# One graph layer with a routed expert layer on one core: the edge sort in four chunks instead of two, positions computed on TensorE, unpadded edge tiles in a ring of 32 buffers with a (tile, block) table, the loops unrolled, and the last row additions made in the output tensor

## The reference

```
xl   = layernorm(x)                                  # x: 3125 x 256, f32
msg  = edge_weight[:, None] * xl[dst]                # 50,000 edges; dst is sorted, src is random
aggr = segment_sum(msg, src, 3125) + (1 + eps) * xl
h    = relu(relu(aggr @ W1 + b1) @ W2 + b2)
x1   = x + normalize(h) * scale + offset
out  = x1 + sum over the two best of 8 experts e of gate_e *
       (gelu(layernorm_e(x1) @ W1_e + b1_e) @ W2_e + b2_e)      # 256 -> 1024 -> 256
```

## Time and profile before

| | |
|---|---|
| median of 3 runs | 1497.83 us (1496.9 to 1498.81) |
| profiled execution, its own time | 1508.24 us |
| span of its trace | 1506.4 us |
| PE / PEld / DVE / ACT / POOL busy | 70% / 50% / 60% / 42% / 51% |
| first edge operation on DVE | 30.08 us |
| first gather | 251.74 us |
| first product of the graph matmuls | 986.69 us |
| start of the last copy's issue | 1493.66 us |

### The profile page before, as it was taken

How to read it: one execution, slowest core, us unless ns; L and a number is a source line. 1 busy time by engine, 2 the same in 40 slices (tenths; PEclk the granted TensorE clock), 3 DMA queues, 4 the chain that set the end, 5 groups by cost and what they waited for, 6 DMA issues and landing times.

```text
span 1506.4 us, 32386 instructions
## 1 busy us (share of the span) xinstructions
PE 1051.3 (70%) x7511; PEld 757.7 (50%) x7512; DVE 899.1 (60%) x2569; ACT 639.5 (42%) x2228; POOL 774.2 (51%) x755
## 2 busy tenths in 40 slices
PE   0003997667667676665665565799549999999994
PEld 0003665445545555333433343478437777777773
DVE  1999997556556666454645455558674545455552
ACT  0633997666666665111111111145244444444441
POOL 3762665555555554666666666532172444434341
PEclk9999998998998989566667666589569999999997
DMA  3020001222222224243434343812211222222224
GB/s 101 23 92 0 0 0 57 77 84 77 79 81 74 79 82 65 84 133 115 136 109 139 115 132 109 180 24 88 94 42 34 38 43 39 43 39 44 39 42 103
DMA packets 61925, 110.50 MB, mean 73 GB/s; under 512 B 11155, under 2 KB 43905, under 8 KB 61828
## 3 DMA queue, kind: packets, MB, share of 16 engines
q0 software_dynamic: 31872, 72.39, 20.5%
q1 hardware_dynamic: 30020, 37.73, 7.8%
HBM read 92.86 MB, written 20.42 MB: 75 GB/s over the span
## 4 chain that ended last, share of the span: by engine, by line
PE 57%; DVE 17%; issue 14%; another core or an unknown queue 5%; DMA 3%; DVEq 2%; SPq 1%; POOL 1%; ACT 0%; POOLq 0%; ACTq 0%
PE bank L613 17%; PE bank L605 10%; PE bank L751 7%; PE bank L738 4%; PE bank L740 4%; PE bank L739 3%; PE bank L753 3%; DVE RA L1230 2%; PE bank L639 2%; DVE Sw L1219 2%; PE bank L693 2%; PE bank L683 1%; DVE RB L1183 1%; DVE Wall L1069 1%
## 5 line engine op out<-in xcount | busy, mean ns | idle before, releaser
L507 POOL DMA_INDIRECT gbuf<-xl_d,idx_slot x440 | 435.4, 990 | 293.8 <-issue 101.1
L613 PE MATMUL bank<-gbuf,Sw 128*128 128x256 f32 x880 | 356.3, 514 | 251.6 <-issue 168.7
L613 PEld LDWEIGHTS bank<-gbuf,Sw 128*128 128x128 f32 x880 | 177.6, 243 | 365.6 <-issue 340.4
L1230 DVE TENSOR_TENSOR RA<-RA,bank 128x256 f32 x440 | 184.3, 419 | 259.4 <-remote 87.8
L605 PE MATMUL bank<-RB 128*128 128x232 f16 (+1 forms) x1960 | 256.6, 270 | 8.3 <-POOL RB L494 2.8
L605 PEld LDWEIGHTS bank<-RB 128*128 128x128 bf16 (+1 forms) x1960 | 185.9, 103 | 78.7 <-issue 29.0
L850 ACT ACTIVATE RB<-RB,pay_slot 128x128 f32<-128x128 f16 x392 | 154.1, 393 | 126.1 <-DVE RB L1176 100.8
L556 POOL DMA_INDIRECT sum_d<-RA,slot_tok x56 | 88.6, 1582 | 204.5 <-DVE RA L1446 185.1
L1008 ACT ACTIVATE RA<-bank,b1T 128x128 f32<-128x128 f32 x448 | 128.0, 368 | 97.6 <-PE bank L740 96.6
L740 PE MATMUL bank<-RA,Wall 128*128 128x128 f16 x896 | 167.2, 223 | 0.0
L738 PE MATMUL bank<-RA,Wall 128*128 128x128 f16 x896 | 166.4, 223 | 0.5 <-issue 0.4
(11 more groups left out here) (225 smaller groups left out, 1570.0 us busy)
## 6 DMA issues: line engine op xcount, KB each, us to landing
stage<-in_L_ffn_W SPq DMA_DIRECT2D x16, 1024.0 KB
gbuf<-xl_d,idx_slot POOLq DMA_INDIRECT x440
out_dram<-sum_d SPq DMA_DIRECT2D x1, 3125.0 KB, 12.3
Wall<-in_x SPq DMA_DIRECT2D x1, 3072.0 KB
xl_d<-Wall SPq DMA_DIRECT2D x1, 3072.0 KB
RB<-in_x SPq DMA_DIRECT2D x1, 3072.0 KB
sum_d<-RB SPq DMA_DIRECT2D x4, 640.0 KB
xn_d<-RA SPq DMA_DIRECT2D x4, 640.0 KB
```

The lines of the kernel that those rows point to most:

```text
L507: pool.indirect_dma_start(out=gbuf[:, j, :], out_offset=None, in_=xl_d, in_offset=bass.IndirectOffsetOnAxis(ap=idx_slot[:, j:j + 1].bitcas ...
L613: mm(bank[5 + j % 2][:, 0:D], Sw[:, j % 4, :], gbuf[:, j, :], start=True, stop=True).then_inc(agg_mm, 1)
L1230: dve.tensor_tensor(a, a, bank[5 + j % 2][:, 0:D], ALU.add).then_inc(agg_added, 1)
```

## The change

Edges are loaded as 128 partitions of 390 values and a remainder column, 391 columns in all. They are cut in four chunks of 72, 96, 110 and 113 columns. Positions come from TensorE: it counts each column's one-hot (`column_counts`, one matmul of one column each), DVE scans the counts and spreads the start of each (column, block) on a diagonal (`spread`), and two matmuls for each group of 20 columns add what is above in the column and the start (`places`); DVE takes the maximum over the blocks. Tiles are no longer padded: a tile of 128 sorted edges may hold several blocks, and a block may span tiles. The pairs (tile, block) are numbered; a chunk of C tiles has SN = C + 24 steps at most, rounded to an even number, so there are 96 + 120 + 134 + 138 = 488 steps of `Sw`, product and addition, and 391 gathers. A table gives two steps (tile, block) in one word; DVE and PE each read it every other step and split it by division and remainder. `Sw` compares a node number against a sliding stretch of a long ramp (`iota_c`), so a row of another block gives zero.

Gathers go into a ring of 32 buffers. Records and table stay in `gbuf` and are read in place by registers; the slot copies of ACT are gone. DVE builds `Sw` three steps ahead (LEAD). Chunk c + 1 is sorted within the steps of chunk c (in its first 63, 87 and 101 steps), and the positions of chunk c + 2 are worked out there too. All of this is unrolled on every engine, with constant waits. DVE takes the layernorm moments of x (25 bn_stats), x is loaded and `xl` stored in five groups, 18 of x's 25 tiles are loaded again before the first gather and 7 after the last step. PREP2 is 3: of the W2 of experts 3 to 7, four are converted within the graph matmuls and one behind the slot tables. The 22 other conversions stand in chunk 3's steps. Rows are added directly in the output tensor, which has 128 spare rows, and the last copy is gone.

```diff
-    C0 = (EC - extra) // 2 // U * U
-    S0 = (C0 + extra + U - 1) // U * U
-    C1 = EC - C0
-    S1 = (C1 + extra + U - 1) // U * U
-    assert C1 == S0 and S1 <= 256
-    COLS, SLOTS, CSTART = (C0, C1), (S0, S1), (0, C0)
...
+    CH = (72, 96, 110, EC - 278)
...
+    SN = [(C + NB - 1 + 1) // 2 * 2 for C in CH]
...
+    RG = 20
+    RING = 32
+    LEAD = 3
+    SR = 8
+    BASE = NB + 1
...
-    PREP2 = (S1 // U - 1 - 2 * NE) // 2
+    PREP2 = 3
+    LATE = (4, 5, 6, 7, 3)
...
+        ring = f32view(Wall, 2 * w2f - RING * D, RING * D)
...
+            for a, t in ((src, e_key), (dst, e_idx), (edge_weight, ew)):
+                sp.dma_start(t[:, 0:EFULL], a[0:EFULL * P].rearrange("(p c) -> p c", c=EFULL)).then_inc(edges_in, 16)
...
+            for g in range(NT // G):
+                full = G - 1 if g == NT // G - 1 else G
+                at = g * G * P
+                sp.dma_start(x_in[:, G * g:G * g + full, :], x[at:at + full * P, :].rearrange("(t p) d -> p t d", p=P)
+                             ).then_inc(x_group[g], 16)
...
+            sp.wait_ge(xl_stored, 16 * (NT // G + 1))
+            sp.wait_ge(acc_set, NT // G)
...
+            sp.dma_start(x1[:, 0:XEARLY, :], x[0:XEARLY * P, :].rearrange("(t p) d -> p t d", p=P)).then_inc(x_early, 16)
...
+            sp.wait_ge(x1_cleared, 1)
+            sp.dma_start(x1[:, XEARLY:NT - 1, :], x[XEARLY * P:FULL, :].rearrange("(t p) d -> p t d", p=P)).then_inc(x_late, 16)
...
+                if g < len(LATE):
+                    sp.wait_ge(w_done, len(CONV) + 2 * g)
+                    load_w2(LATE[g])
...
-            sp.dma_start(out, sum_d[0:N, :]).then_inc(out_done, 16)
...
-            with pool.Fori(0, C0 // U) as i:
-                for j in HI_ON_POOL:
...
-                    pool.tensor_scalar(hi16[:, j, 0:S0], iota_h[:, 0:S0], pay_slot[:, j // HALF, j % HALF, 1:2], None,
...
+            pool.wait_ge(acc_set, NT // G)
+            pool.wait_ge(xl_stored, 16 * (NT // G + 1))
+            for c in range(NCH):
+                pool.wait_ge(recs_taken, c + 1)
...
+                        pool.wait_ge(agg_mm, SB[of] + min(t - RING - T0[of] + NB - 1, SN[of] - 1) + 1)
+                    pool.indirect_dma_start(
+                        out=ring[:, t % RING * D:(t % RING + 1) * D], out_offset=None, in_=xl_d,
+                        in_offset=bass.IndirectOffsetOnAxis(ap=rec_i[:, t:t + 1].bitcast(U32), axis=0),
+                    ).then_inc(gathered[t % RING], 16)
...
+            def column_counts(c, k):
+                pe.wait_ge(oh_built, sum(groups(j) for j in range(c)) + k + 1)
+                for t in group_cols(c, k):
+                    m = mm(ranks[0:NB, t:t + 1], e_oh[c % 2][:, t, :], one_h[:, 0:1], start=True, stop=True)
...
+                o = bank[4 + n % 2][:, 0:w]
+                mm(o, above_big[:, :], e_oh[c % 2][:, cols[0]:cols[-1] + 1, :].rearrange("p t b -> p (t b)"), start=True, stop=False)
+                mm(o, ones[0:NB, :], spread_d[n % 3][:, 0:len(cols), :].rearrange("p t b -> p (t b)"),
+                   start=False, stop=True).then_inc(place_mm, 1)
...
-                for k, left in enumerate((node[:, :, 1], node[:, :, 0], wt[:, :, 1], wt[:, :, 0], lo_rest[:, s, :])):
...
+                for j, left in enumerate((node[:, :, 1], node[:, :, 0], wt[:, :, 1], wt[:, :, 0], lo_rest[:, s, :])):
+                    m = mm(bank[j // 4][:, j % 4 * P:j % 4 * P + CH[c]], left, hi16[:, s, 0:CH[c]],
...
+            def ring_slot(c, i):
+                if i % 2 == 0:
+                    pe.wait_ge(steps_ready, c + 1)
+                    h = (SB[c] + i) // 2
+                    words[h] = pe.value_load(step_tab[0:1, h:h + 1], min_val=0, max_val=(BASE * CH[c]) ** 2 - 1)
+                word = words[(SB[c] + i) // 2]
+                tile = (word // BASE) % CH[c] if i % 2 == 0 else word // (BASE * CH[c] * BASE)
+                return (tile + T0[c]) % RING * D
+            def agg_step(c, i):
+                n = SB[c] + i
+                at = pe.snap(ring_slot(c, i))
+                pe.wait_ge(sw_built, n + 1)
+                if n >= 2:
+                    pe.wait_ge(agg_added, n - 1)
+                if i < CH[c]:
+                    t = T0[c] + i
+                    pe.wait_ge(gathered[t % RING], 16 * (t // RING + 1))
+                mm(bank[2 + n % 2][:, 0:D], Sw[:, n % 4, :], ring[:, bass.ds(at, D)], start=True, stop=True).then_inc(agg_mm, 1)
...
-                act.activation(xl[:, t, :], x_in[:, t, :], ACT.Copy, accum_out=mean1[:, t:t + 1]).then_inc(sums_done, 1)
...
-                        words(C0 + U * i + j, j, 1)
-                        words(C0 + U * i + j + 1, j + 1, 1)
...
-                link(dve.tensor_copy(cprev[:, 1:B], cum[:, 0:B - 1, T - 1]))
...
+            def column_hots(c, k):
+                cols = group_cols(c, k)
+                n, c0 = len(cols), T0[c] + k * RG
+                dve.tensor_tensor(e_oh[c % 2][:, cols[0]:cols[-1] + 1, :],
...
+                C = CH[c]
+                dve.wait_ge(col_counts, sum(groups(j) for j in range(c + 1)))
+                link(dve.tensor_tensor_scan(incl[:, 0:C], ones[0:NB, 0:C], ranks[0:NB, 0:C], 0.0, ALU.mult, ALU.add))
...
-                for b in range(B):
-                    m = dve.scalar_tensor_tensor(out=work[:, b, :], in0=cum[:, b, :], scalar=first[:, b:b + 1], in1=oh[:, b, :],
...
-                link(dve.tensor_reduce(pos, work.rearrange("p b t -> p t b"), AX_X, ALU.add))
...
+                link(dve.tensor_tensor(step_v[:, 0:S], row25[:, 1:1 + S], ranks[0:1, 192:192 + S], ALU.subtract))
...
+                link(dve.scalar_tensor_tensor(out=step_tab[:, SB[c] // 2:(SB[c] + S) // 2], in0=two[:, :, 1],
+                                              scalar=float(BASE * CH[c]), in1=two[:, :, 0], op0=ALU.mult, op1=ALU.add))
...
+                if n >= 3:
+                    dve.wait_ge(place_mm, n - 2)
+                dve.tensor_tensor(spread_d[n % 3][:, 0:w, :],
+                                  base[:, cols[0]:cols[-1] + 1].rearrange("p (t a) -> p t a", a=1).to_broadcast([NB, w, NB]),
...
+                dve.tensor_reduce(pos_f[:, cols[0]:cols[-1] + 1], bank[4 + n % 2][:, 0:w * NB].rearrange("p (t b) -> p t b", b=NB),
+                                  AX_X, ALU.max).then_inc(place_taken, 1)
...
+                link(dve.tensor_scalar(pos_i[:, 0:C], pos_i[:, 0:C], 7, None, ALU.arith_shift_right))
...
-                last = dve.tensor_scalar(lo_hot[:, s, :], iota_h[:, 0:P], p_[0], None, ALU.is_equal)
...
-                if chunk or s not in HI_ON_POOL:
-                    last = dve.tensor_scalar(hi16[:, s, 0:S], iota_h[:, 0:S], p_[1], None, ALU.is_equal)
...
+                    dve.bn_stats(stats[:, t, :], x_in[:, t, :]).then_inc(stats_done, 1)
...
+                lane, tile = epay[:, n, 0:1], epay[:, n, 1:2]
+                dve.tensor_scalar(lo_hot[:, s, :], iota_h[:, 0:P], lane, None, ALU.is_equal).then_inc(hot_built, 1)
+                if c == 0 and n % 2:
+                    dve.tensor_scalar(lo_rest[:, s, :], iota_h[:, 0:P], lane, epay[:, n, 4:5], ALU.is_equal, ALU.mult)
+                dve.tensor_scalar(hi16[:, s, 0:CH[c]], iota_h[:, 0:CH[c]], tile, None, ALU.is_equal).then_inc(sort_built, 1)
...
-                word = dve.value_load(blk_tab[c][0:1, bass.ds(group, 1)], min_val=0, max_val=NB ** HALF - 1)
-                return [(word // NB ** k) % NB for k in range(HALF)]
...
+            def step_word(c, i):
+                h = (SB[c] + i) // 2
+                if h not in words:
+                    words[h] = dve.value_load(step_tab[0:1, h:h + 1], min_val=0, max_val=(BASE * CH[c]) ** 2 - 1)
+                return words[h]
+            def block_of(c, i):
+                word = step_word(c, i)
+                return word % BASE if i % 2 == 0 else (word // (BASE * CH[c])) % BASE
+            def tile_of(c, i):
+                word = step_word(c, i)
+                return (word // BASE) % CH[c] if i % 2 == 0 else word // (BASE * CH[c] * BASE)
...
+                r = [rec_f[:, bass.ds(t + T0[c], 1), k] for k in range(2)]
+                dve.tensor_scalar(Sw[:, n % 4, :], iota_c[:, bass.ds(block_of(c, i) * P, P)], r[0], r[1],
+                                  ALU.is_equal, ALU.mult).then_inc(sw_built, 1)
...
+                dve.wait_ge(agg_mm, n + 1)
+                if n:
+                    dve.wait_ge(agg_added, n)
+                a = RA[:, bass.ds(block_of(c, n - SB[c]) * D, D)]
+                dve.tensor_tensor(a, a, bank[2 + n % 2][:, 0:D], ALU.add).then_inc(agg_added, 1)
...
+                for i in range(SN[c]):
+                    if c + 2 < NCH:
+                        rank_part(c + 2, i - 2)
+                    if c + 1 < NCH:
+                        while k < CH[c + 1] and sort_tick(c, k) <= i:
+                            sort_build(T0[c + 1] + k)
+                            k += 1
+                        if i == sort_tick(c, CH[c + 1] - 1) + 3:
+                            records(c + 1)
```

(70 more changed lines are left out.)

1057 lines of the change are left out of this document (493 added, 564 removed).

## The result

The changed kernel takes 1823.65 us (median of 4 runs, 1820.83 to 1827.0), the kernel before 1497.37 beside it: ratio 1.219, 95% interval 1.215 to 1.223. I had forecast 1286, range 1175 to 1410, and slower at 7%: both range and direction are wrong. The span of the trace is 1825.1 us.

What follows compares the result with a forecast made beforehand. The aggregation, nearly half the span, was taken as bound by order, not an engine's throughput. First gather at 130 us plus 656.5 gives 786.7; with 507.8 behind, 1294.5 us of span, 1286 on the median's scale, range 1175 to 1410.

Steps and rivals of the forecast that it cites:

- 251 x 1.45 = 364 us: Aggregation: 251 steps with the next chunk's sort beside them, each priced at DVE's work, 1.45 us.
- if the steps wait in pairs for PE: Aggregation steps in the new profile: a sign named in advance that the forecast is wrong; no size given.
- 237 x 1.10 us: Aggregation: 237 steps without sorting, 0.69 us of DVE plus 0.41 for the word, 261 us.
- the stream of instructions stalls: Rival, unrolled code: a 7.26 us hole each 16 steps, 30 holes cost 219 us, 1505 us; chance 7%.
- it stood at the jump: Old aggregation loop: argument against stalls, the 7.26 us hole came at the loop's return, none that long between jumps.
- The words: Aggregation, reading table words on DVE: 0.2 us a sorting step, 0.41 in the others.
- paid in full: Rival, aggregation: word reads fully exposed, 0.53 us a step on DVE, 1395 us, or 1445 with PE's; chance 22%.
- cost nothing: Rival, aggregation: word reads are free and gathers become the bound, 1179 us; chance 20%.
- Conversions: Aggregation: 22 weight conversions at 1.25 us on DVE add 27 us.
- First gather: Stage up to the first gather: 251.7 to about 130 us, bounds 105 to 155, a gain of 122 us.
- Behind: After the aggregation: 519.7 to 507.8 us; last copy saves 12.9, conversions in graph matmuls cost 3, routing saves 2.
- theory C: Aggregation, put forward after the result: products at TensorE's 1.2 GHz set the pace, so four columns' lead changes under 30 us.

Runs made afterwards that it cites:

- The lead: Sort one-hots built four columns ahead of PE's products; side by side, with late W2 halves and paired conversions in both, 1540.7 us with it, 1808.4 without.
- e5_lead4_late: Changed kernel with sort one-hots four columns ahead and the eight late W2 halves at steps where their loads can have landed; ratio 1.027 to the kernel before.
- e1_lead4: Changed kernel with sort one-hots built four columns ahead; ratio 1.034 to the kernel before, 1419.3 us on a chip where that takes 1375.2.
- held-back gathers: Changed kernel with tile t gathered only when step t - 8 of its chunk is done, no other edit; ratio 1.184 to the kernel before.
- e9_lead4_pairs: As e5_lead4_late, with chunk 3's 22 conversion halves in pairs three steps apart; 1540.7 us, ratio 1.020 to the kernel before.
- the last run: Four-column lead, late W2 halves, paired conversions and held-back gathers, with 12 of 16 matmuls of each W1 half left out; 1478.9 us, one run.
- e10_paced: As e9_lead4_pairs, with tile t gathered only when step t - 8 of its chunk is done; 1508.8 us, ratio 1.002 to the kernel before.

## Why the prediction was wrong, step by step

**"That is 251 x 1.45 = 364 us"** is the step that failed. I priced a sorting step as the sum of what DVE has to do, as if every other engine's part lay beside it, although I had written that the stage was "bound by order, not by an engine's throughput". Two streams that run in step must be read with their distance: which column does DVE build while PE multiplies column k? In the changed kernel both loops use `sort_tick(c, k) <= i`; DVE's stands in the diff above, and this is PE's:

```diff
+                    agg_step(c, i)
+                    if c + 1 < NCH:
+                        while k < CH[c + 1] and sort_tick(c, k) <= i:
+                            sort_step(c + 1, k)
```

So the distance is nothing, and the way DVE, ACT, PE, DVE is walked once for every two steps. Measured: 2.88 us for 1.45 in chunk 1, 720 us over the three chunks for 364. The lead brings back some 270 us; with it a sorting step takes 1.85 us on a slower chip (e5_lead4_late) and 1.46 on the fast one (e1_lead4); that the last meets my 1.45 is in part luck, since I forecast from rows of a slower chip. The whole stage took 485 us more than forecast: 356 in sorting steps, 50 in free steps of chunks 0 to 2, 63 in chunk 3, the rest where chunks change. I had listed the sign ("if the steps wait in pairs for PE") and given it no chance.

**"237 x 1.10 us"**: the pace between holes was right. In chunk 2's free steps, from the timeline of DVE:

```profile
1042.24 0.41 DVE L1270 TENSOR_TENSOR RA<-RA,bank 128x256 f32 x1
...
1043.04 0.41 DVE L1270 TENSOR_TENSOR RA<-RA,bank 128x256 f32 x1
...
1044.47 0.41 DVE L1270 TENSOR_TENSOR RA<-RA,bank 128x256 f32 x1
...
1045.26 0.41 DVE L1270 TENSOR_TENSOR RA<-RA,bank 128x256 f32 x1
```

2.22 us for two steps (1043.04 to 1045.26), 1.11 each. The mean of 1.62 contains stretches of 3 to 7 us a step, and held-back gathers bring it down to 1.26 to 1.35. These stretches look like my rival "the stream of instructions stalls", but a run of gathers beside the instructions decides, not their newness alone. In chunk 0 two additions stand 23 us apart in the result's trace (164.31 and 187.44) and 26 in e5_lead4_late and e9_lead4_pairs.

I had also misread the place of the 7.26 us hole, on which that rival's "it stood at the jump" rests. In the first 192 steps of chunk 1 the loop of the kernel before comes round behind every 32nd step, and the additions around such a place are:

```profile
756.22 0.42 DVE L1230 TENSOR_TENSOR RA<-RA,bank 128x256 f32 x1 [1.33 <-PE bank L613]
...
764.16 0.42 DVE L1230 TENSOR_TENSOR RA<-RA,bank 128x256 f32 x1 [7.26 <-issue]
...
766.94 0.42 DVE L1230 TENSOR_TENSOR RA<-RA,bank 128x256 f32 x1
...
768.88 0.42 DVE L1230 TENSOR_TENSOR RA<-RA,bank 128x256 f32 x1
```

The hole (764.16) stands before the 29th of 32 steps, as in rows 7; the jump lies between the last two rows, 1.94 us apart with a conversion of 1.22 us between them. So the jump took DVE less than 1 us here, and it is the straight stretch that has the hole. POOL issues gathers at 1.26 us up to 761.19 in it, as in the changed kernel's stretches; that the cause is the same is not shown.

**The words**: 0.41 a free step was forecast; the run without DVE's word shows 0.3, without both 0.4 to 0.5. In sorting steps 0.2 was forecast, and with the lead it is between nothing and 0.16. Rival "paid in full" (0.53 in every step) does not hold, nor "cost nothing". The 20 us that I added for a read of 0.6 us do not come out of my figures: 146 us for 244 reads are no more than the 147 that the sum already held (251 x 0.2 + 237 x 0.41). The read itself, by the instructions of line L1240:

```profile
L1240 DVEq TENSOR_LOAD <-gbuf x244: 3/303/706, 148.9 to 1286.0; - x122
```

0.30 us in the median (minimum, median, maximum in ns). The Trainium skill ("DMA: Bandwidth & Descriptors", section "Latency and other measured facts") gives about 600 ns; here the table lies in on-chip memory, and the measurement decides.

**Conversions, "27 us"**: mis-sized. Chunk 3 took 1.76 a step where free steps have 1.26 without holes: some 0.5 x 138 = 69 us for 22. I had counted DVE's 1.25 us and left out the 8 products that PE makes one after the other for a W1 half (16 matmuls in the trace), in the order ahead of the next step, 35 to 38 us of it by the estimate from the last run.

**First gather, 130 forecast, 149.3 measured.** DVE began at 7.66 (forecast 14), placing took 31.5 us (26), the moments 11 (14). POOL's accumulators stretched DVE as forecast; the timeline shows it beside the same operation undisturbed:

```profile
50.98 0.25 DVE L1208 TENSOR_SCALAR Wall<-iota_h,Wall 128x128 f16<-128x128 f16 x1
...
59.02 3.52 DVE L1208 TENSOR_SCALAR Wall<-iota_h,Wall 128x128 f16<-128x128 f16 x1
```

The end was set by ACT, which I had at 119 us because I let it work without waits: it waited for one-hots that DVE wrote late in the stretch beside POOL, and could not make them up at 0.73 us a column.

**Behind, -12 forecast, +14 measured.** The stage with the late halves took 21 us more and not 3: 14 by an ordered wait for a load, as e5_lead4_late shows, and 7 for which no run has the cause. The missing copy gave 7.4 us of the 12.9: before, 26.8 us passed from the last product of the experts' first layer (L738, L836 after) to the end, now 19.4 (1805.7 to 1825.1). In the timeline of POOL the last scatter is issued at 1815.78:

```profile
1815.78 1.55 POOL L608 DMA_INDIRECT out_dram<-RA,slot_tok  x1 [3.12 <-DMA out_dram<-RA,slot_tok]
```

9.3 us pass from there to the end of the span. That the copy had covered a part of them is argued. The expert stage is unchanged, as forecast (350.5 and 351.1 us).

**The clock.** I took PE's 1.03 us a step at a clock of 0.65 as a fact of the stage. It is also a result of the order: with the lead and nothing else changed, chunk 1's window has 0.80 in place of 0.51 (level 1.2 GHz nearly throughout), and a matmul of the step's product takes 502 ns in place of 702. As theory C had it, with the lead worth under 30 us, it is refuted. But a part of the lead's gain can have gone through the clock, and no run holds the clock fixed. Chunk 0 does not speak against that, though its steps are the slowest, 3.61 us, and its clock is given as 1.00. Window and group of its sorting steps in the result's trace:

```profile
154.00:378.60 224.60, 134.44 (x728) 77.21 (x727) 91.80 (x361) 87.73 (x282) 63.88 (x68) 1.00 0.14 40
```

```profile
L708 PE MATMUL bank<-Wall,Sw 128*128 x125 | 74.6, 699 | 14.5 <-issue 12.3 <-DVE Sw L1261 1.1 <-DVE RA L1270 0.4
```

The same matmul takes 699 ns here as in chunk 1 at 0.51, and 429 in chunk 2 of e1_lead4 at 0.99. So for this stretch the granted clock does not tell how fast PE worked.

## What to carry to other kernels

When a software pipeline is rewritten, list for each pair of producer and consumer how many steps lie between them, before and after, and price a step as the longest way around the ring divided by the steps in it; sums of busy time give only a floor. A rewrite can win each part that it was written for and lose all of it at one index. And a term for "beside other work" needs the order on that engine: a conversion, or an ordered wait for a load, costs what stands behind it.

## What the runs showed of the hardware

The kernel before took 1375 us on one chip and 1494 to 1506 on the others.

The figure of the granted clock can stand at 1.00 over a stretch in which matmuls take as long as at 0.51 (699 and 702 ns): read a matmul's mean time beside it.

In the traces of the slower chips there are stretches in which TensorE or VectorE takes one instruction at a time, at distances of 0.7, 1.4, 2.1 or 2.8 us, for up to 35 us, while GpSimd issues gathers every 1.26 us. In e1_lead4's trace, on the fast chip, PE runs 288 matmuls from 148 to 185 us, where e9_lead4_pairs has 60. Held-back gathers remove most of it; 8 us (155.68 to 163.91) are left in e10_paced.

What is delayed is not shown. Instruction fetches are a natural guess, and the trace has them as DMA queues of their own, q8 and q14. For e9_lead4_pairs from 158 to 195 us it lists one queue; from 195 to 211 us, when the pace is back, it lists these two:

```profile
q0 software_dynamic: 1277, 3.46, 32.9%
```

```profile
q8 instruction: 2, 0.03, 1.0%
q14 instruction: 1, 0.01, 0.2%
```

Nothing of the instruction queues moves in the slow stretch itself. That speaks against a fetch under way in it; a fetch that waits for its start is not excluded. The Trainium skill ("Runtime: NRT & Kernel Launch", section "Instruction fetch mechanics") has straight code's supply as mostly hidden; whether these stretches go against it depends on that open point.
